# An LSTM over 1024 steps on one core: the input projection x·Wx taken out of the prologue and spread over the time loop

## What is computed

```python
# x: (2, 1024, 256), cond = h0: (2, 256), W: (256, 256), Wx, Wh: (256, 1024), b: (1024,)
ys = cond / 16;  d = rsqrt((ys * ys) @ (W * W) + 1e-8)
x = x + ((x * ys[:, None, :]) @ W) * d[:, None, :]
xW = x @ Wx + b                       # for all 1024 steps
h, c = cond, 0
for t in range(1024):
    a = xW[t] + h @ Wh                # 2 x 1024: the gates i, f, o, g
    c = sigmoid(f) * c + sigmoid(i) * tanh(g)
    h = sigmoid(o) * tanh(c)
    hs[t] = h
return x + hs
```

## Time and profile before

| | us |
|---|---|
| median of three runs | 2076.63 (2074.16 to 2077.5) |
| the profiled execution | 2076.23 |
| its span | 2074.4 |
| prologue, up to the first matmul of the loop | 88.84 |
| one step of the loop at 0.50 of the clock | 1.93 |

### The profile page before, as it was taken

The page is one execution under the profiler, slowest core; times in us unless marked ns, Lnnn a source line. Parts: engine busy times, 40 slices in busy tenths (PEclk is TensorE's granted clock), DMA queues, the critical chain, the costliest instruction groups (busy, mean ns, idle before and its releaser), DMA issues.

```text
span 2074.4 us, 141184 instructions
## 1 busy us (share of the span) xinstructions
PE 1876.6 (90%) x57580; PEld 1735.5 (84%) x57580; DVE 1269.5 (61%) x8384; ACT 697.6 (34%) x5149; POOL 498.7 (24%) x1291
## 2 busy tenths in 40 slices
PE   8999999999999999999999999999999999999997
PEld 5588888888888888888888888888888888888887
DVE  3366666666666666666666666666666666666665
ACT  2233333333333333333333333333333333333333
POOL 1122222222222222222222222222222222222221
PEclk9855555555555555555555555555555555555555
DMA  2000000000000000000000000000000000000000
GB/s 86 2 1 1 1 1 1 1 1 1 1 1 1 1 1 1 1 1 1 1 1 1 1 1 1 1 1 1 1 1 1 1 1 1 1 1 1 1 1 1
DMA packets 20368, 6.67 MB, mean 3 GB/s; under 512 B 17532, under 2 KB 19848, under 8 KB 20360
## 3 DMA queue, kind: packets, MB, share of 16 engines
q1 hardware_dynamic: 20088, 6.30, 1.2%
q10 hardware_dynamic: 272, 0.26, 0.0%
HBM read 4.46 MB, written 2.10 MB: 3 GB/s over the span
## 4 chain that ended last, share of the span: by engine, by line
PE 73%; DVE 12%; ACT 9%; issue 5%; DMA 0%; SPq 0%; POOLq 0%; POOL 0%; DVEq 0%
PE psum L293 73%; DVE psum L584 10%; ACT scan_in L661 9%; DVE psum L577 2%; DMA x_rows<-in_x_dram 0%; SPq L188 0%; PE psum L316 0%; ACT xw L640 0%; SPq L183 0%; SPq L184 0%; POOLq L56 0%; POOL y_cols L244 0%; DVE y_rows L598 0%; DVE y_rows L603 0%; DVE psum L575 0%
## 5 line engine op out<-in xcount | busy, mean ns | idle before, releaser
L293 PE MATMUL psum<-h_parts,wh_p 128*128 128x2 f16 (+1 forms) x45056 | 1370.8, 166 | 0.0
L293 PEld LDWEIGHTS psum<-h_parts,wh_p 128*128 128x128 f16 x45056 | 1286.8, 104 | 16.8
L293 PE MATMUL psum<-ring,ident_b 128*128 128x4 bf16 (+2 forms) x12288 | 491.1, 168 | 186.2 <-DVE psum L584 184.5
L293 PEld LDWEIGHTS psum<-ring,ident_b 128*128 128x128 bf16 x12288 | 407.3, 105 | 271.0 <-DVE psum L584 268.4
L658 ACT ACTIVATE sig_f<-psum 128x4 f32<-128x4 f32 x1024 | 178.2, 174 | 1127.9 <-DVE psum L575 1127.9
L575 DVE TENSOR_REDUCE psum<-psum 128x4 f32<-128x8 f32 x1024 | 179.2, 175 | 389.8 <-PE psum L293 389.8
L232 POOL CAST ring<-xw 128x64 bf16 (+1 forms) x256 | 120.7, 471 | 1149.5 <-POOLq L270 1124.9
L587 DVE SCALAR_TENSOR_TENSOR h_parts<-scan_h 128x4 f16<-128x4 f32 x1024 | 176.1, 172 | 248.2 <-ACT scan_h L667 248.2
L663 ACT ACTIVATE scan_h<-psum 128x2 f32<-128x2 f32 x1024 | 177.2, 173 | 134.6
L590 DVE TENSOR_TENSOR_SCAN h_parts<-scan_h,h_parts 128x12 f16<-128x12 f32 x1024 | 188.4, 184 | 35.1
L577 DVE TENSOR_REDUCE psum<-psum 128x4 f32<-128x8 f32 x1024 | 179.2, 175 | 39.4
(11 more groups left out here) (75 smaller groups left out, 212.0 us busy)
## 6 DMA issues: line engine op xcount, KB each, us to landing
out_dram<-y_rows SPq DMA_DIRECT2D x512, 4.0 KB
x_rows<-in_x_dram SPq DMA_DIRECT2D x4, 512.0 KB, 7.1
wh_sb<-in_L_cond_Wh_dram SPq DMA_DIRECT2D x1, 1024.0 KB, 10.4
wx_sb<-in_L_cond_Wx_dram SPq DMA_DIRECT2D x1, 1024.0 KB, 12.1
w_sb<-in_L_cond_weight_dram ACTq DMA_DIRECT2D x1, 256.0 KB, 2.8
small_rows<-in_cond_dram SPq DMA_DIRECT2D x1, 2.0 KB
small_rows<-in_L_cond_b_dram SPq DMA_DIRECT2D x1, 4.0 KB
```

The source lines that it names most:

```text
L293: return nc.tensor.matmul(out_, lhs, rhs, start=first, stop=last, skip_group_check=True)
```

## The change

The prologue makes xW only for the first 128 steps and one 17th piece more. The work is cut into items: one item is 128 steps of one chunk and one sequence, so 16 items (ITEMS) are a block of 128 steps, and there are 128 items and 128 turns. The prologue does the first 17 (LEAD); turn i makes item i + 17, modulo 128. `xw` is stored by items. An item is 12 matmuls of 128 columns (`project`): 2 chunks of k, 2 f16 parts of Wx (`wx_p`), 3 bf16 parts of x (`x_p`), with weights and columns addressed by registers. One stands in each step behind the inputs of F, one more in every even step behind the inputs of O. At the end of a turn ACT reads the bank into `xw` (a new activation of 128 columns behind the tanh of the eighth step, which raises `x_read`), and before its first matmul of a turn PE waits for `x_read` and for `x_split`. The inputs of F move from behind `c_done` to in front of it, behind a new wait for `f_act`. POOL splits 8 steps of x into bf16 parts in each turn (`split_x`, 4 operations), and waits for `x_read` once a turn.

For that the prologue takes a second maximum, of |Wx|, before the first scales can be made; DVE splits x of steps 128 to 271 (4 operations, 576 elements a partition); ACT writes two more copies, of Wx; the subtractions for the second parts of Wh and Wx stand on DVE, at the end; and one half of the x projection stands behind the scales. Banks: the sums of F, G and O move into the gates' own banks, which leaves one free for the items.

```diff
+LEAD = 17
+AHEAD = 2 * LEAD
             # POOL, in the turn
+                    if half == 0:
+                        pool.wait_ge(x_read, i + 1)
+                        pool.sem_inc(pool_seen, 1)
+                    split(half, i + 1)
+                    if half == 0:
+                        split_x(i)
             # PE, prologue
-            for n in range(1, NB):
-                project_x(n)
+            project_x(1, [0])
             bank = start_group(("scales",))
...
+            project_x(1, range(1, B))
...
-            for n in range(NB):
-                for b in range(B):
-                    for m in range(M):
-                            last = mm(bank[:, :], wx_sb[:, k, m * P:(m + 1) * P], xt[:, k, b, n * BANK:(n + 1) * BANK], k == 0, k == K - 1)
+            for v in range(LEAD):
+                    last = mm(bank[:, 0:P], wx_sb[:, k, m * P:(m + 1) * P], xt[:, k, b, block * P:(block + 1) * P], k == 0, k == K - 1)
             # PE, loop
+                item = pe.snap((i + LEAD) % NI)
+                weights = pe.snap(((item // B) % M) * P)
+                rows = pe.snap((item % B) * T + (item // ITEMS) * P)
+                terms = [(k, w_part, x_part) for k in range(K) for w_part in range(2) for x_part in range(3)]
+                def project(n):
+                    k, w_part, x_part = terms[n]
+                    return mm(banks[X_BANK][:, 0:P], wx_p[:, w_part, k, bass.ds(weights, P)],
+                              x_p[:, x_part, k, :, :].rearrange("p b t -> p (b t)")[:, bass.ds(rows, P)], n == 0, n == len(terms) - 1)
                 for u in range(UNROLL):
                     if u % HALF == 0:
                         pe.wait_ge(ring_full, 2 * i + u // HALF + 1)
+                    if u == 0:
+                        pe.wait_ge(x_split, i + 1)
+                        pe.wait_ge(x_read, i + 1)
+                    pe.wait_ge(f_act, t + u + 1)
+                    input_apart(GATE_F, u, 0, K)
+                    last = project(done)
+                    done += 1
+                    if done == len(terms):
+                        last.then_inc(x_mm, 1)
                     pe.wait_ge(c_done, t + u + 1)
-                    input_apart(GATE_F, u, 0, K)
                     input_apart(GATE_G, u, 0, K)
                     input_together(GATE_I, I_BANK, u, 0, K)
                     pe.wait_ge(o_act, t + u + 1)
...
+                    if u % 2 == 0:
+                        project(done)
+                        done += 1
                     pe.wait_ge(h_hi, t + u + 1)
             # DVE, prologue
+            nc.vector.tensor_reduce(wmax[:, 1:2], wx_sb[:, :, :], AX.XY, ALU.max, apply_absolute_value=True).then_inc(s_wmax, 1)
+            add_projection(0, range(B))
...
+            link(nc.vector.tensor_copy(x_p[:, 0, :, :, soon], xt[:, :, :, soon]))
+            link(nc.vector.tensor_tensor(x_rest[:, :, :, :], xt[:, :, :, soon], x_p[:, 0, :, :, soon], ALU.subtract))
+            link(nc.vector.tensor_copy(x_p[:, 1, :, :, soon], x_rest[:, :, :, :]))
+            nc.vector.tensor_tensor(x_p[:, 2, :, :, soon], x_rest[:, :, :, :], x_p[:, 1, :, :, soon], ALU.subtract).then_inc(x_split, 1)
...
+            nc.vector.tensor_tensor(wh_p[:, 1, :, :], wh_s[:, :, :], wh_p[:, 0, :, :], ALU.subtract).then_inc(s_wh_lo, 1)
+            nc.vector.tensor_tensor(wx_p[:, 1, :, :], wx_s[:, :, :], wx_p[:, 0, :, :], ALU.subtract).then_inc(s_wx_lo, 1)
             # ACT, before the loop and at the end of the turn's eighth step
+            act.sem_inc(x_read, 1)
...
                     nc.scalar.activation(scan_h[:, :, 2], cell[:, :, 2], ACT.Tanh).then_inc(t_done, 1)
+                    if u == UNROLL - 1:
+                        act.wait_ge(x_mm, i + 1)
+                        act.sem_inc(act_seen, 1)
+                        nc.scalar.activation(xw[:, bass.ds(item, 1), :].rearrange("p n t -> p (n t)"), banks[X_BANK][:, 0:P], ACT.Identity,
+                                             bias=bias_s[:, bass.ds(chunk, 1)], scale=x_unit[:, :]).then_inc(x_read, 1)
```

More of the change, by code:

```diff
@@ L135, in cond_resid_lstm @@
         s_wh_hi, s_wh_lo, s_start = sem("s_wh_hi"), sem("s_wh_lo"), sem("s_start")
+        s_wx_hi, s_wxs, s_wx_lo = sem("s_wx_hi"), sem("s_wxs"), sem("s_wx_lo")
+        x_split, x_mm, x_read, act_seen = sem("x_split"), sem("x_mm"), sem("x_read"), sem("act_seen")
         s_table = sem("s_table")
@@ L226, in settle, with split @@
                 pool.sem_inc(s_pool, -1)
-            def split(half, t0):
-                src = by_gate(xw_t[:, :, bass.ds(t0, HALF)])
+            def split(half, turn):
+                t0 = pool.snap(turn * UNROLL + half * HALF) if not isinstance(turn, int) else turn * UNROLL + half * HALF
+                src = by_gate(xw_of_step(t0))
                 res = by_gate(rest[:, :, :])
@@ L260, in _, with split_x @@
             split(0, 0)
-            split(1, HALF)
-            for s, v in last_read("xw"):
-                pool.wait_ge(s, v)
+            split(1, 0)
+            def split_x(turn):
+                t0 = pool.snap(((turn + AHEAD) % NI) * UNROLL)
+                now = xt[:, :, :, bass.ds(t0, UNROLL)].rearrange("p k b t -> p (k b) t")
+                res = x_rest[:, :, :, 0:UNROLL].rearrange("p k b t -> p (k b) t")
+                part = [x_p[:, q, :, :, bass.ds(t0, UNROLL)].rearrange("p k b t -> p (k b) t") for q in range(3)]
+                nc.gpsimd.tensor_copy(part[0], now).then_inc(s_pool, 1)
+                settle()
+                nc.gpsimd.tensor_tensor(res, now, part[0], ALU.subtract).then_inc(s_pool, 1)
+                settle()
+                nc.gpsimd.tensor_copy(part[1], res).then_inc(s_pool, 1)
+                settle()
+                nc.gpsimd.tensor_tensor(part[2], res, part[1], ALU.subtract).then_inc(x_split, 1)
             with pool.Fori(0, NI - 1) as i:
@@ L373, in _ @@
             pe.wait_ge(s_identb, 1)
+            pe.wait_ge(s_wx_hi, 1)
+            pe.wait_ge(s_wx_lo, 1)
+            pe.wait_ge(c_done, 1)
             def apart(gate, first, last):
@@ L379, in together @@
             def together(bank, first, last):
-                return banks[bank][:, B * first:B * last].rearrange("p (c b) -> p c b", b=B)
+                start = 2 * CB if bank == I_BANK else 0
+                return banks[bank][:, start + B * first:start + B * last].rearrange("p (c b) -> p c b", b=B)
             def in_ring(gate, u, part, first, last):
@@ L523, in _ @@
             nc.vector.tensor_scalar(bias_s[:, :], small[:, B * K:NSMALL], scales[:, 0:1], None, ALU.mult).then_inc(s_bias, 1)
+            nc.vector.tensor_tensor(x_unit[:, :], scales[:, 0:1], scales[:, 3:4], ALU.mult).then_inc(s_bias, 1)
+            add_projection(1, range(1, B))
             bank = group(("h0wh",))
```

148 lines of the change are left out of this document (82 added, 66 removed).

## The result

| | before | after |
|---|---|---|
| median, us | 2077.07 | 2285.68 (2283.35 to 2295.65) |
| the profiled execution | 2076.23 | 2295.65 |
| its span | 2074.4 | 2293.8 |
| first matmul of the loop | 88.84 | 54.56 |
| from there to the end | 1985.6 | 2239.2 |

The changed kernel takes 1.1017 times as long, 95% interval 1.1000 to 1.1034. The prediction was 2171 us with a range of 2108 to 2238: the sign was right, and the time was outside the range. The loop starts 34.3 us earlier, and is 253.6 us longer: 2.00 us for each of the 127 turns that wait, where 1.05 had been forecast.

A forecast was written before the change was run, and what follows sets the result against it. It took PE's f32 matmuls to bound the prologue's x·Wx, and a chain through scan, tanh and products the 1024 steps of 1.93 us. 2076.2 − 38.0 (earlier loop) + 133 (stalls) = 2171 us, range 2108 to 2238.

The forecast's parts named there:

- start of the loop: Prologue: the loop's first matmul comes at 50.8 us and not 88.84, 38.0 us earlier, bounds 33 to 41.
- wait for the read, and PE's work behind it: At a turn's start the first product comes 1.05 us later; 133 us in 127 turns, bounds 51 and 229.
- the read's path: From the scan's end (E) through the tanh and ACT's 0.32 us read to the signal at PE, at E+0.54.
- its five: PE's register instructions at a turn's start: x_split wait, three before the first projection, one before the second; 0.45 us taken.
- upper bound for the stall: At a turn's start: a read of 0.5 us behind the whole tanh and 1.0 for registers, some 1.8 us.
- the forecast's own case: One stall a turn in the loop, 2115 to 2240 us by itself, chance 0.70.
- POOL's extra work: Four operations of 32 elements a turn in the loop, some 2.1 us plus register work, against idle stretches of 5.37 and 1.89.
- PE's own part behind the wait: At a turn's start, once the read is signalled: 12 inputs and two projections 0.53 us, register instructions 0.45.
- One stall a turn: Each turn from the second on (127) waits at its start for the read ending the turn before, 1.05 us each.
- No stall: Rival: the x_read wait is met before PE gets there, so only the prologue's gain stays, 2038 us; chance 0.05.
- every step pays: Rival: steps 3, 5 and 7 each late by 0.1 to 0.2 us, 38 to 77 us; 2210 to 2250; chance 0.13.
- that rival: The projections' added columns raise the loop's clock to 1.0, steps of 1.90 us and not 1.93; 2123 us; chance 0.10.

## Why the prediction was wrong in size

**The sum as measured.** By the profiled executions:

| term | forecast | measured | shown by |
|---|---|---|---|
| start of the loop | −38.0 | −34.3 | timeline |
| wait for the read, and PE's work behind it, 127 turns | +133 (1.05) | +221 (1.74) | rows above; the kernel without subtractions gives (2208.7 − 1985.6)/127 = 1.76 |
| scans and other DVE work lengthened by POOL | 0 | +30.5 (0.24) | the same kernel; the mean of the scan gives 22 of it |

2076.2 − 34.3 + 221 + 30.5 = 2293.4, against 2295.65 measured. Without the third term it is 2263, over the range already.

**The step that failed: the read's path, E+0.54 in the forecast and E+1.22 measured.** Three terms of it were too small, and together they make 0.68 of the missing 0.69:
- Its start, "between 0.06 and 0.18 after E+0.04", was E+0.52. The register instructions of the read (0.17 and 0.06 on ACTq) run only when the tanh ahead, which waits for `c_done`, has gone. I had costed register work on PE and none on ACT. With constant addresses the read starts at E+0.21, near the E+0.16 forecast.
- Its length, 0.32 between 8 and 512 columns, was 0.46. The line was drawn between two kinds of activation: the one of 8 columns reads PSUM alone, the one of 512 a bias and a scale from tiles as well, as the read does. From 128 to 512 columns of that kind it is 0.46 to 0.78, or 0.83 ns a column. No run changes the operands alone.
- From its end to PE it took 0.24 and not 0.06, with and without registers on ACT or PE. The 0.06 was read from a scan and a matmul that waits for it itself. Here a semaphore instruction waits: it starts 0.04 us behind the read's end, the register instruction with the wait for `x_split` comes next, and the matmul only then, 0.10 behind that one's start (the rows of L475 and L476). The forecast had this one register instruction in its five, but not the second stop.

My upper bound for the stall, 1.8, did hold the measured 1.74 to 1.76. What took the time out of the range was that I gave the forecast's own case only up to 2240 and the range less. On top comes a term that wasn't in the sum at all.

**The term that was missing: POOL beside the scan.** "POOL's extra work" was costed only by whether it has time. Before, the mean of the scan is 193 ns: POOL's subtractions stand beside a quarter of the scans, but start too far ahead to lengthen one. In the changed kernel they start just ahead of a scan about five times in three turns (181 of 870 scans). It was in no step and in no rival.

**What held.**
- PE's own part behind the wait: 0.53 for inputs and projections and 0.45 for registers, 0.98; measured 2.21 − 1.22 = 0.99. The run with constant addresses puts 0.50 of it on the register work, the kernel without the read 0.48. That the 0.45 fits is partly luck: it was priced as five instructions of 0.09 to 0.12 with some overlap, and in the trace the three of the address arithmetic alone make 0.47, the one before the second projection nothing, and those with the waits the 0.18 of the term above. The rule that the prediction took from the Trainium skill, page Perfetto Trace Analysis, section Sequencer Loop (an engine instruction is pushed into a queue, a control instruction starts executing in ucode), agrees with the trace: the address arithmetic starts at 1012.42, behind the met wait. But the prediction tied the bare register work to the late wait, and that is too narrow: with the wait for `x_read` gone altogether it still costs 0.48, because PE's stream is only a third of a microsecond ahead at the end of a turn.
- One stall a turn, 127 of them, for the reason given. "No stall" and "every step pays" fell: steps 2 to 8 take 1.93 unless a scan is hit.
- The clock stayed at 0.50 in the loop, so that rival fell as well.

**The prologue.** The forecast had the first matmul of the loop at 50.8 and it came at 54.56. The items were costed at 7.9 us, with 1.5 in reserve for the clock. In the changed kernel's execution they took 10.54 and the halved projection 6.65, at clocks of 0.74 (37 to 48 us) and 0.53 (26 to 33 us), after PE had been idle for 2.4 us. In the execution without the read the same instructions took 7.84 and 3.70, at 1.00 in both, after 2.6 us idle:

```profile
27.65 3.70 PE L321 MATMUL psum<-xt,wy 128*128 128x512 f32 x8
...
34.68 7.84 PE L321 MATMUL psum<-xt,wx_sb 128*128 128x128 f32 x68
```

So the price at the full clock was right, and the clock of this stretch is not a property of the kernel: in the twelve executions profiled with it (two of them with the subtractions on POOL) the loop starts between 46.6 and 54.6. The end of the prologue was right in size (6.6 us from the last item to the loop, 6.9 measured) and wrong in kind: DVE's subtractions end at 52.71, and it is POOL's split, slowed by them, that PE waits for.

## What to carry to other kernels

A wait placed on a loop's critical chain costs what stands in front of it and behind it on both engines, register work and the signal's way included, so price the address arithmetic of every instruction that stands behind a late semaphore, and do it early, in pieces, where the engine has a hole. Where one engine needs the answer of another, ask for it a few steps after it is made: moving the projections two steps on, and the address arithmetic into the holes, turned 10% slower into 1.4% faster with the same work. An added instruction on an engine with time to spare isn't free if it slows the engine on the chain: compare the lengths of the chain's own operations before and after, and look at what starts just ahead of the longer ones.

## What the runs showed that was not expected

- The address arithmetic of one item costs 0.48 to 0.50 us a turn on PE, and makes the read of ACT start 0.31 us later.
- An activation of 128 columns from PSUM with bias and scale from tiles takes 0.46 us. PE starts 0.24 us behind its end, through a semaphore and a register instruction of its stream, and 0.06 behind a scan of DVE for which the matmul itself waits.
- A subtraction of POOL from two SBUF tiles that starts 0.01 to 0.14 us ahead of a DVE scan of 12 columns lengthens it from 0.19 to as much as 0.33 us; one that starts 0.28 ahead, or behind it, doesn't. A cast of POOL 0.02 ahead lengthens DVE's L664 by 0.04. The other way round, DVE's subtraction of 2048 columns (2.3 us) stretches a POOL cast of 64 columns from 0.47 to 2.39 us.
- After 2.4 to 2.6 us of idle PE, the same f32 matmuls ran at a clock of 1.00 in one execution and of 0.53 in another.
